# Attention over 1,024 steps: one score maximum in eight taken over a raised sum, value products in one piece and in another place

## The reference, cut to what matters

```python
A1 = jnp.einsum('bhqd,bhkd->bhqk', Q1, K1) * scaling
A2 = jnp.einsum('bhqd,bhkd->bhqk', Q2, K2) * scaling
attn = jax.nn.softmax(A1, axis=-1) - lamb * jax.nn.softmax(A2, axis=-1)
out = jnp.einsum('bhqk,bhkd->bhqd', attn, V)
```

## Time and profile before

| what | value |
|---|---|
| median of three runs | 3233.37 us |
| span of the profiled execution | 3232.2 us |
| TensorE matmul busy | 3089.3 us |
| VectorE busy | 2735.8 us |
| ScalarE busy | 2502.6 us |
| GpSimd busy | 453.2 us |

### The profile page before, as it was taken

How to read it: one execution, slowest core, us unless ns; L and a number is a source line. 1 busy time by engine, 2 the same in 40 slices (tenths; PEclk the granted TensorE clock), 3 DMA queues, 4 the chain that set the end, 5 groups by cost and what they waited for, 6 DMA issues and landing times. The chain is left out here.

```text
span 3232.2 us, 72457 instructions
## 1 busy us (share of the span) xinstructions
PE 3089.3 (96%) x29281; PEld 1389.4 (43%) x29282; DVE 2735.8 (85%) x2902; ACT 2502.6 (77%) x4689; POOL 453.2 (14%) x654
## 2 busy tenths in 40 slices
PE   8999999999999999999999999999999969999995
PEld 4333333333333333333333333333332658999995
DVE  3599999999999999999999999999998683433443
ACT  3269999999999999999999999999999552333333
POOL 2000000000000000000000000000000464555554
PEclk9989999999999999999999999999999979999997
DMA  6520101111020101011010101021002561222224
GB/s 159 124 45 15 35 21 30 30 34 28 15 35 24 28 15 35 29 30 28 28 28 18 34 21 28 15 51 28 15 9 83 206 227 34 38 38 36 36 37 124
DMA packets 101213, 152.92 MB, mean 47 GB/s; under 512 B 21592, under 2 KB 64464, under 8 KB 99248
## 3 DMA queue, kind: packets, MB, share of 16 engines
q1 hardware_dynamic: 85008, 130.03, 16.2%
q0 software_dynamic: 15904, 18.66, 3.6%
HBM read 88.35 MB, written 60.29 MB: 46 GB/s over the span
## 5 line engine op out<-in xcount | busy, mean ns | idle before, releaser
L1005 DVE TENSOR_REDUCE half_max<-scores 128x2 f32<-128x1024 f32 x2016 | 2297.4, 1219 | 10.5 <-PE scores L759 4.8
L930 ACT ACTIVATE probs<-bank 128x512 f32<-128x512 f32 x4012 | 2142.3, 595 | 142.5 <-PE bank L772 45.5
L831 PE MATMUL bank<-probs,V 128*32 128x256 f32 x16384 | 1309.6, 391 | 44.2 <-ACT probs L930 42.4
L759 PE MATMUL scores<-K,Q 48*128 48x512 f16 x4032 | 793.9, 388 | 3.0 <-SPq L542 2.2
L772 PE MATMUL bank<-Q,K 50*128 50x512 f16 x4012 | 789.7, 380 | 0.0
L831 PEld LDWEIGHTS bank<-probs,V 128*32 128x32 f32 x16384 | 322.5, 108 | 583.2 <-issue 517.7
L759 PEld LDWEIGHTS scores<-K,Q 48*128 48x128 f16 x4032 | 194.2, 93 | 834.6 <-DVE half_max L1005 532.2
L772 PEld LDWEIGHTS bank<-Q,K 50*128 50x128 f16 x4012 | 371.2, 94 | 183.0 <-ACT probs L930 4.2
L660 POOL TENSOR_SCALAR max_parts<-row_max 128x16 f16<-128x16 f32 x64 | 16.2, 253 | 2066.3 <-DVE row_max L1011 2066.3
L1604 ACT ACTIVATE h<-u 128x1024 f32<-128x1024 f32 x71 | 75.0, 1057 | 260.8 <-DVE u L1648 260.8
L1565 PE MATMUL pre<-xgT,w 128*128 128x128 f32 x2272 | 265.3, 275 | 2.3 <-ACT xgT L1598 2.3
(11 more groups left out here) (195 smaller groups left out, 1204.8 us busy)
## 6 DMA issues: line engine op xcount, KB each, us to landing
attended<-att SPq DMA_DIRECT2D x64, 256.0 KB, 2.5
W<-in_L_ffn_w_dram SPq DMA_DIRECT2D x16, 1024.0 KB, 6.4
Q<-q_parts SPq DMA_DIRECT2D x96, 128.0 KB, 6.6
K<-k_parts SPq DMA_DIRECT2D x96, 128.0 KB, 6.9
values<-attended SPq DMA_DIRECT2D x6, 2048.0 KB, 9.2
q_parts<-parts SPq DMA_DIRECT2D x64, 128.0 KB, 2.4
k_parts<-parts SPq DMA_DIRECT2D x64, 128.0 KB, 2.4
xT<-in_x_cols_dram SPq DMA_DIRECT2D x8, 512.0 KB, 4.9
```

The lines of the kernel that those rows point to most:

```text
L759: mm = nc.tensor.matmul(scores[:, b, h, :], Q[p][r, c, up, t * P:(t + 1) * P], K[p][r, up, kc * TC:(kc + 1) * TC], start=True, stop=True)
L831: mm = nc.tensor.matmul(banks[att_bank[s // KB]][32 * u:32 * u + 32, q], V[wp][:, wk, u // 2, :], probs[:, 4 * s % RING + u, q], start=(wk ...
L930: nc.scalar.activation(probs[:, i % RING, :], banks[tile_bank[i]][:], ACT.Exp, scale=SCALE).then_inc(exp_done, 1)
L1005: nc.vector.tensor_reduce(half_max[lc % 2][:, :, up, t, kc], scores[:, b], AX.X, ALU.max).then_inc(max_done[b], 1)
```

## The change: what it does

In 62 of the 64 chunks, two of the 16 steps (`is_duo`) no longer take two maxima over 1024 columns. For such a step TensorE makes the scores of the first 512 keys (one `score_pair` instead of two) and, in two banks of the ring, their difference to the scores of the next 512 keys (`score_gaps`: a matmul with the negated queries and one with the queries, added up in PSUM). ScalarE makes max(0, difference) into `gaps` (`raise_gaps`, Relu). VectorE's `tensor_tensor_reduce` adds `gaps` to the first scores and takes the maximum (a + max(0, b - a) is the larger of a and b), once for each half of the array. The places of the second pair in `half_max` are set to -3e38 once. GpSimd negates part of the queries (`negate_q`), twice for each of 16 groups.

`weigh` is no longer cut in two: four matmuls over 512 columns, between tiles u0, u1 and the second `score_pair`. The tables of banks and counts are made by a loop over all steps. The diff, cut to its core:

```diff
+        def is_duo(step):
+            return BLANKED * KB <= step < STEPS and step % KB in DUO_AT      # DUO_AT = (4, 12), BLANKED = 2
...
+            tiles = [(j + LAG, u) for u in range(UNITS)]
+            if j >= 0 and is_duo(j + 1 + AHEAD):
+                tiles += [("gap", j + 1 + AHEAD, h) for h in range(2)]
+            for tile in tiles:
+                nth[tile], TAKEN = TAKEN, TAKEN + 1
+                if tile[0] == "gap" or tile[0] < PAIRED:
+                    bank = ring[at_ring % 3]
+                    tile_bank[tile], tile_after[tile] = bank, last.get(bank)
+                    last[bank], at_ring = ("taken", nth[tile]), at_ring + 1
...
+            def score_gaps(step):
...
+                gap_banks = [bank_of(("gap", step, h)) for h in range(2)]
+                for part in range(2):
+                    for h in range(2):
+                        r = slice(HALF * h, HALF * h + KR)
+                        q = minus_q[p][r, c, up, :] if part == 0 else Q[p][r, c, up, t * P:(t + 1) * P]
+                        mm = nc.tensor.matmul(gap_banks[h][:], q, K[p][r, up, (kc + part) * TC:(kc + part + 1) * TC],
+                                              start=(part == 0), stop=(part == 1))
...
             for u in range(UNITS):
-                q = slice(TC // 2 * part, TC // 2 * (part + 1))
-                mm = nc.tensor.matmul(banks[att_bank[s // KB]][32 * u:32 * u + 32, q], V[wp][:, wk, u // 2, :],
-                                      probs[:, 4 * s % RING + u, q],
+                mm = nc.tensor.matmul(banks[att_bank[chunk]][32 * u:32 * u + 32, :], V[g % 2][:, wk, u // 2, :],
+                                      probs[:, UNITS * step % RING + u, :],
...
-                        weigh(j, 0)
-                        if item < STEPS:
-                            score_pair(item, ahead // KB, ahead % KB * 2)
-                        transposed(it, j, lc, 0)
-                        weigh(j, 1)
-                        if item < STEPS:
-                            score_pair(item, ahead // KB, ahead % KB * 2 + 1)
-                        transposed(it, j, lc, 1)
+                if item < STEPS:
+                    score_pair(item, 0)
+                transposed(step + LAG, 0)
+                weigh(step)
+                if item < STEPS and not is_duo(item):
+                    score_pair(item, 1)
+                transposed(step + LAG, 1)
+                if is_duo(item + 1):
+                    score_gaps(item + 1)
...
+            def raise_gaps(step, before):
...
+                for h in range(2):
+                    act.wait_ge(scoresT_ready, nth["gap", step, h] + 1)
+                    nc.scalar.activation(gaps[:, h, :], banks[tile_bank["gap", step, h]][:], ACT.Relu).then_inc(exp_done, 1)
...
+                        nc.vector.tensor_tensor_reduce(
+                            out=gaps[:, h, :], in0=scores[:, k % 2, h, :], in1=gaps[:, h, :], scale=1.0, scalar=BLANK,
+                            op0=ALU.add, op1=ALU.max, accum_out=half_max[lc][:, h, up, t, kc:kc + 1]).then_inc(max_done[k % 2], 1)
```

More of the change, by code:

```diff
@@ L442, in stage_attend @@
         CT = UNITS * KB
[L444 to L462, removed]
+        DUO_TILE = TPC // 2
+        DUO_AT = (4, 12)
@@ new lines, in stage_attend, with scores_at @@
+        BLANKED = 2
+        def is_duo(step):
+            return BLANKED * KB <= step < STEPS and step % KB in DUO_AT
+        def scores_at(step, b=0):
+            n = 2 * (step % KB) + b
+            return n // (TPC * KC), n // KC % TPC, n % KC
+        for d in DUO_AT:
+            assert scores_at(d)[1] == DUO_TILE
+        item_at, ends_at, ITEMS = {}, [], 0
+        for step in range(STEPS):
+            for b in range(1 if is_duo(step) else 2):
+                item_at[step, b], ITEMS = ITEMS, ITEMS + 1
+            if step % KB == KB - 1:
+                ends_at.append(ITEMS - 1)
@@ L464, in at @@
+        for n in range(len(att_bank), CHUNKS):
+            raise AssertionError(n)
         def at(h, i):
@@ L771, in scores_of @@
+            def scores_of(step, u):
+                p, kb, c = step // KB // CH % 2, step % KB, step // KB % CH
                 r = slice(HALF * (u % 2), HALF * (u % 2) + KM)
-                nc.tensor.matmul(banks[tile_bank[i]][:], K[p][r, u // 2, kb * P:(kb + 1) * P],
+                nc.tensor.matmul(bank_of((step, u))[:], K[p][r, u // 2, kb * P:(kb + 1) * P],
                                  Q[p][r, c, u // 2, :], start=True, stop=True).then_inc(scoresT_ready, 1)
@@ L793, in transposed, with weigh @@
                     for u in range(2 * b, 2 * b + 2):
-                        scores_of(it * 4 * RS, j + LAG, u, it * RC + lc)
+                        scores_of(step, u)
+            def weigh(step):
+                chunk, g, wk = step // KB, step // KB // CH, step % KB
+                if wk == 0 and att_after[chunk] is not None:
+                    pe.wait_ge(exp_done, max(att_after[chunk], nth[step, UNITS - 1]) + 1)
+                else:
+                    pe.wait_ge(exp_done, nth[step, UNITS - 1] + 1)
+                if step % (CH * KB) == 0:
+                    pe.wait_ge(v_copied, g + 1)
+                for u in range(UNITS):
+                    mm = nc.tensor.matmul(banks[att_bank[chunk]][32 * u:32 * u + 32, :], V[g % 2][:, wk, u // 2, :],
+                                          probs[:, UNITS * step % RING + u, :],
+                                          start=(wk == 0), stop=(wk == KB - 1), skip_group_check=True)
+                mm.then_inc(pv_done, 1)
             for i in range(PRE, AHEAD):
                 for b in range(2):
-                    score_pair(i, i // KB, i % KB * 2 + b)
+                    score_pair(i, b)
                     if i >= AHEAD - LAG:
@@ L801, in _ @@
                             pe.wait_ge(max_loaded[0], MXD + 1)
-                        for u in range(2 * b, 2 * b + 2):
-                            scores_of(0, i - (AHEAD - LAG), u)
+                        transposed(i - (AHEAD - LAG), b)
                     for n in range(1 if i >= AHEAD - LAG else 2):
[L805 to L829, removed]
-                                q = slice(TC // 2 * part, TC // 2 * (part + 1))
-                                mm = nc.tensor.matmul(banks[att_bank[s // KB]][32 * u:32 * u + 32, q], V[wp][:, wk, u // 2, :],
-                                                      probs[:, 4 * s % RING + u, q],
[L833 to L843, removed]
-                        weigh(j, 0)
-                        if item < STEPS:
-                            score_pair(item, ahead // KB, ahead % KB * 2)
-                        transposed(it, j, lc, 0)
-                        weigh(j, 1)
-                        if item < STEPS:
-                            score_pair(item, ahead // KB, ahead % KB * 2 + 1)
-                        transposed(it, j, lc, 1)
@@ new lines, in _ @@
+                        nc.tensor.matmul(banks[att_bank[0]][:], K[0][0:KR, b, 0:P], Q[0][0:KR, 0, b, :], start=True, stop=True)
+            for step in range(STEPS):
+                item, chunk = step + AHEAD, step // KB
+                if item < STEPS and item % (CH * KB) == 0:
+                    g = item // (CH * KB)
+                    pe.wait_ge(qk_loaded[g % 2], QKD * ((g + 1) // 2))
+                if step % KB == KB - LAG and chunk + 1 < CHUNKS:
+                    pe.wait_ge(max_loaded[(chunk + 1) % 2], MXD * ((chunk + 1) // 2 + 1) + 1)
+                if step == SETUP_AT:
+                    pe.wait_ge(exp_done, nth[PAIRED - 1, UNITS - 1] + 1)
+                    pe.wait_ge(rw_mulled, 1)
+                    for f in range(KD):
+                        nc.tensor.transpose(turn_x[:, 0, f * E:(f + 1) * E], rw_scaled[:, f * P:(f + 1) * P], ident[0:E, 0:E])
+                    pe.wait_ge(rb_ready, 1)
+                    pe.wait_ge(consts_set, 3)
+                    nc.tensor.matmul(lgp[:, 0, :], rb_ones[:], rb_diag[:], start=True, stop=True).then_inc(rw_turned, 1)
+                if item < STEPS:
[7 more added lines that the diff above has]
+                    score_gaps(item + 1)
@@ L945, in _ @@
[L945 to L960 removed]
+                    i = (UNITS * step + 2 * b) % RING
@@ new lines, in paired_exps @@
+                    act.wait_ge(scoresT_ready, nth[step, 2 * b + 1] + 1)
+                    nc.scalar.activation(probs[:, i:i + 2, :], scores[:, b], ACT.Exp, scale=SCALE).then_inc(exp_done, 2)
+            def raise_gaps(step, before):
+                if before is not None:
+                    k = item_at[before, 0]
+                    act.wait_ge(max_done[k % 2], 2 * (k // 2 + 2))
+                for h in range(2):
+                    act.wait_ge(scoresT_ready, nth["gap", step, h] + 1)
+                    nc.scalar.activation(gaps[:, h, :], banks[tile_bank["gap", step, h]][:], ACT.Relu).then_inc(exp_done, 1)
@@ new lines, in copy_att @@
+            def copy_att(chunk):
+                act.wait_ge(pv_done, (chunk + 1) * KB + 1)
```

(20 more changed lines are left out.)

200 lines of the change are left out of this document (111 added, 89 removed).

## The result

The changed kernel takes **3714.53 us** (median of four runs, 3712.68 to 3716.64) against 3232.79 us for the kernel before beside it: a ratio of 1.149 (1.147 to 1.151), or 482 us more. 3762 was predicted, with 3590 to 3860 as the range.

The account below looks back on a forecast made before the run. Before, VectorE 1.14, ring 1.13 and TensorE 1.11 us stood side by side per half step; after, the wait from u2 to u1 binds. 3232.2 + 378 + 11 + 140 = 3761, so 3762 us forecast, range 3590 to 3860.

Parts of the forecast that it names:

- The way from u2 to u1: Ring of three banks: u1 needs u2's exponential, so 1.13 us from u2 to u1, with TensorE standing still in between.
- The step: A plain step of four transposed tiles: 1.13 + 0.32 + 1.00 + 0.22 = 2.67 us against 2.293, +378 us over 1003 steps.
- product to scores: The whole value product (`weigh`) before the second scores: 0.57 us for 256 columns plus 0.43, so 1.00 us.
- from a pair's first tile to its exponential takes 0.48 us: Delay from a pair's first transposed tile to its exponential when ScalarE is free; 0.48 us, part of the 1.13.
- The ends of chunks: A chunk's first `weigh` waits for u3's exponential of the step before: 0.17 x 62 = +11 us.
- The gap tiles: In duo steps they wait for u2's bank and delay the next u1 through the Relu: 1.13 x 124 = +140 us.
- VectorE at nothing: VectorE does at most 2.28 us of a 2.67 us step, so its saving of some 100 us is worth nothing.
- the upper price of 0.90: One `tensor_tensor_reduce` on VectorE priced from above, as 0.688 plus a small reduction of 0.212 us; 0.688 was taken.
- Faster: Rival, chance 0.05: VectorE stays the bound and the ring does not bind; 62 chunks save 99 us, 3134 us.
- Only the gaps cost: Rival, chance 0.06: VectorE bounds every step except the 124 duo steps, which add 186 us: 3420 us.
- Clock: Rival, chance 0.05: TensorE's clock falls to 1.2 GHz; a tenth of the steps add 150 us (3910), all 1530.
- wait mostly for VectorE: Reading of the profile before: the plain scores' weight loads were taken to wait mostly for VectorE.

Follow-up runs that it names:

- run 2: The changed kernel with tiles u2 and u3 made ahead of the second plain scores, same work in another order: 3519.95 us.
- run 5: The changed kernel with one more, long satisfied wait on ScalarE ahead of u2's exponential in each step: 3820.37 us.
- run 7: The changed kernel without duo steps and with a fourth bank in the ring, taken from left-out plain scores; VectorE's work kept: 3249.32 us.
- run 1: The changed kernel without its duo steps, all maxima as before, value products still in one piece: 3562.18 us.
- run 10: The changed kernel with one more unused maximum over 1024 columns on VectorE in each of the 124 duo steps: 3713.84 us.
- run 4: The changed kernel with the order of before, half a value product ahead of each score pair, duo steps kept: 3432.5 us.

## Why the prediction was right, point by point

- **The way from u2 to u1** was the cause, and the runs tie it down from three sides: work taken out of the way from u1 to u2 shortens the step by its length (run 2), 0.06 us put into the exponential's start lengthens it by 0.06 (run 5), and with a fourth bank the wait and the loss are gone with the products unmoved (run 7; at least 92 us of that gain are beyond what the left-out scores explain).
- **The step was put at 2.67 us and takes 2.61.** Three of its terms held: u1 to the product 0.32, product to scores 1.00, scores to u2 0.22 (0.23). The term that was mis-sized is "from a pair's first tile to its exponential takes 0.48 us": it is 0.41. The 0.48 was read at a pair u0 u1, whose first exponential stands behind a second wait (for `pv_done`) in ScalarE's queue; u2's has one wait. Run 5 puts the second wait there and gets 0.47. Over 1003 steps that is some 60 us too much.
- **The ends of chunks** were put at 11 us. Run 1's 329 us are 1003 x (2.61 - 2.293) = 318 and these 11.
- **The gap tiles** were put at 1.13 us each and cost 1.23 (run 1). They start 0.14 us after the end of u2's exponential, where a single tile follows by 0.055.
- Without the 0.06 us a step the sum would have been 3762 - 60 = 3702, and with 0.10 us more for each of 124 duo steps 3714. (The upper end of the range, 3860, lies 7 us above all upward prices taken together, 3762 + 54 + 37.)
- **VectorE at nothing** held: run 10 adds 140 us of work without effect. Its price was within the bounds, near the lower one: two sums start 0.62 us apart (1341.38, 1342.00). The Trainium skill (VectorE: DVE Perf Modes, section Two Vector instructions with no wait between them) counts an operation that also writes its accumulator as two instructions; the trace agrees and shows the second as an accumulator read of 0.08 us. It starts together with the next sum (1342.00), so the upper price of 0.90 doesn't follow from it.
- **The rivals.** "Faster" falls with run 1 and run 10. "Only the gaps cost" falls with run 1. "Clock" was real but small: three falls of 3.4 us in the stage. The Trainium skill (TensorE: Matmul & The Clock Gate, section A second HAM failure mode: psum-queue depth-cycling) tells of short idles between groups of matmuls with which the clock goes to and fro. Run 5 agrees, with 20 falls in its stage.
- **One reading was wrong, without harm.** The scores of the half step in the earlier trace rows did not wait for VectorE. They start 0.57 us after the product (2485.45 to 2486.02), as in run 4 (1223.43 to 1224.00), where the same 0.41 us before the weight load stand against "issue". So the "wait mostly for VectorE" of the earlier trace rows is mostly time in which the product runs: 0.41 us in each of 4010 / 2 = 2005 half steps are 822 of the 828.2 us. No term of the sum rests on it.

```profile
2485.45 0.64 PE L831 MATMUL bank<-probs,V 128*32 128x256 f32 x8
```

## What to carry to other kernels

With three buffers in turn for pairs of tiles, what counts is the distance between pairs, not TensorE's total: the largest piece of work that stands between two pairs adds to the buffer's round trip instead of covering it, so a piece of 1.32 us (u1 to the product's end) and a round trip of 1.07 us (u2 to u1, run 2) can't give a step under 2.39 us, however little else there is. Cut such a piece, and put the parts where they cover the round trips; then look at the places where the order is broken (here the end of a chunk), since turning the order by one position was worth 14 us. A saving on the busiest engine is worth what is left when the work that buys it has been put on the shared buffers.

## What was not expected of the hardware

- A second wait that is long satisfied, ahead of an instruction that then waits for a tile, made ScalarE start 0.06 us later after that tile (0.41 against 0.47 us, run 5).
- With 0.06 us a step more of idle time, TensorE's clock fell 20 times in the stage instead of three, each time behind a duo step, and some 46 us went beyond the 60 expected. A matmul repeated in the idle time gave 22 us back: 19 falls, but each of 3.4 us.
